# Relu attention on one core: scores and sums grouped by key block, four products for seven

## The reference

```python
Q = jnp.einsum('bnd,hed->bhne', x, Wq)          # 8 heads, 128 wide
K = jnp.einsum('bnd,hed->bhne', x, Wk)
V = jnp.einsum('bnd,hvd->bhnv', x, Wv)
scores = jnp.einsum('bhne,bhme->bhnm', Q, K)
causal = jnp.tril(jnp.ones((n, n), dtype=bool))
sim = jnp.where(causal, jax.nn.relu(scores), 0.0) / n      # n = 512
head_out = jnp.einsum('bhnm,bhmv->bnv', sim, V)            # summed over heads
s = x + head_out
```

## Time and profile before

| | |
|---|---|
| median of 3 runs | 770.13 us (767.93 to 770.13) |
| profiled execution, its own time | 770.88 us |
| its span, first to last instruction | 769.1 us |
| TensorE busy | 726.7 us, 94% |
| VectorE busy | 485.3 us, 63% |
| ScalarE busy | 422.8 us, 55% |
| POOL busy | 228.5 us, 30% |
| mean granted TensorE clock | 0.993 of full |

### The profile page before, as it was taken

The page is one execution under the profiler, slowest core; times in us unless marked ns, Lnnn a source line. Parts: engine busy times, 40 slices in busy tenths (PEclk is TensorE's granted clock), DMA queues, the critical chain, the costliest instruction groups (busy, mean ns, idle before and its releaser), DMA issues.

```text
span 769.1 us, 17574 instructions
## 1 busy us (share of the span) xinstructions
PE 726.7 (94%) x6166; PEld 577.8 (75%) x6172; DVE 485.3 (63%) x1084; ACT 422.8 (55%) x1540; POOL 228.5 (30%) x308
## 2 busy tenths in 40 slices
PE   4899999999999899999999999989999999999996
PEld 3677888878886677777767778868688787777866
DVE  6433333369886787777877775474655647556575
ACT  2444444432224567677666767374756647566473
POOL 1130000000003797776766761161303111010000
PEclk9999999999999999999999999899999999999999
DMA  8702000000001323333333330000000000000001
GB/s 251 290 1 57 0 0 0 0 0 0 0 1 43 91 63 74 87 88 86 81 85 78 81 92 21 1 9 11 14 4 17 7 11 1 1 0 0 0 1 56
DMA packets 26192, 32.73 MB, mean 43 GB/s; under 512 B 7184, under 2 KB 15888, under 8 KB 25488
## 3 DMA queue, kind: packets, MB, share of 16 engines
q1 hardware_dynamic: 24848, 29.27, 13.8%
q0 software_dynamic: 1280, 2.62, 1.3%
HBM read 12.98 MB, written 2.10 MB: 20 GB/s over the span
## 4 chain that ended last, share of the span: by engine, by line
PE 56%; issue 11%; POOL 10%; DVE 7%; POOLq 7%; ACT 5%; DMA 2%; DVEq 2%; SPq 1%; ACTq 0%
PE ps L733 9%; PE ps L745 9%; PE ps L1001 7%; PE ps L1061 6%; POOL early L569 5%; POOLq L577 5%; PE ps L1028 4%; PE ps L1044 4%; PE ps L720 4%; PE ps L714 4%; PE ps L1037 2%; POOL stage L576 2%; POOLq L579 2%; POOL early L588 2%; ACT stage L1301 2%
## 5 line engine op out<-in xcount | busy, mean ns | idle before, releaser
L569 POOL TENSOR_TENSOR early<-stage 128x512 f32<-128x512 f32 x64 | 91.0, 1442 | 55.4 <-DVE stage L1654 38.5
L1301 ACT ACTIVATE stage<-ps,nmB 128x128 f32<-128x128 f32 x256 | 89.9, 380 | 29.7 <-DVE nmB L1687 29.7
L1362 ACT ACTIVATE early<-ps,nmC 128x128 f32<-128x128 f32 (+1 forms) x224 | 77.5, 363 | 40.9 <-DVE dnC L1750 40.8
L745 PE MATMUL ps<-stage 128*128 128x128 f32 (+2 forms) x448 | 86.2, 321 | 1.4 <-DVE stage L1548 1.2
L733 PE MATMUL ps<-stage,early 128*128 128x128 f32 (+2 forms) x448 | 86.4, 321 | 0.0
L733 PEld LDWEIGHTS ps<-stage,early 128*128 128x128 f32 x448 | 65.2, 191 | 24.5 <-issue 15.5
L745 PEld LDWEIGHTS ps<-stage 128*128 128x128 f32 x448 | 65.5, 191 | 12.1 <-issue 1.9
L1028 PEld LDWEIGHTS ps<-stage,early 128*128 128x128 f32 x448 | 56.2, 193 | 22.6 <-issue 22.5
L1246 ACT ACTIVATE stage<-ps 128x512 f32<-128x512 f32 x64 | 31.4, 490 | 65.2 <-PE ps L733 65.2
L1543 DVE COPY stage<-ps 128x512 f32<-128x512 f32 x32 | 22.1, 692 | 69.4 <-PE ps L720 69.0
L1745 DVE TENSOR_REDUCE nmC<-ps 128x4 f32<-128x512 f32 (+1 forms) x56 | 36.4, 651 | 43.8 <-PE ps L1028 43.6
(11 more groups left out here) (199 smaller groups left out, 1486.2 us busy)
## 6 DMA issues: line engine op xcount, KB each, us to landing
early<-early SPq DMA_DIRECT2D x256, 64.0 KB, 2.0
x<-in_x SPq DMA_DIRECT2D x4, 256.0 KB, 3.5
stage<-in_cq SPq DMA_DIRECT2D x1, 1024.0 KB, 6.2
stage<-in_ck SPq DMA_DIRECT2D x1, 1024.0 KB, 8.2
stage<-in_cv SPq DMA_DIRECT2D x1, 1024.0 KB, 10.2
stage<-in_co SPq DMA_DIRECT2D x1, 1024.0 KB, 12.1
early<-in_wqk SPq DMA_DIRECT2D x1, 1024.0 KB, 14.0
xrows<-xhat SPq DMA_DIRECT2D x1, 1024.0 KB, 5.6
```

The costliest lines, as they stand in the source:

```text
L569: pool.tensor_tensor(to, a, b, (ALU.subtract, ALU.add)[f]).then_inc(rot_in, 1)
L745: t = pe.matmul(ps[:, b, q0:q1], vN[:, b % 2, m, :], simA[:, b % 2, s, at:at + q1 - q0], start=False, stop=False, skip_group_check=True)
L1301: t = act.activation(pB[:, u % 2, at, :], ps[:, 4 + h, i * P:(i + 1) * P], ACT.Exp, bias=nmB[:, u % 2, at:at + 1], accum_out=rsB[:, u % 2, ...
L1362: act.activation(pC[:, k, hg, 0:n], ps[:, 5 + k, hg * P:hg * P + n], ACT.Exp, bias=nmC[:, k, hg:hg + 1], accum_out=rsC[:, k, hg:hg + 1])
```

## The change

Step s now holds products of a whole key block: step 0 is key block 0 with all 512 queries, step 1 is key block 1 (384) and key block 3 (128), step 2 is key block 2 (256). Four products stand where seven stood, with the same ten blocks. Each bank then holds diagonal and later blocks together. ScalarE's `a_relu` takes the later blocks out (384, 256 and 128 columns), and only when it has done does VectorE's `a_diag` take the diagonal ones (one, two and one block). So ScalarE has three such instructions a unit, VectorE three in place of one, and sums s waits for VectorE alone. Where VectorE's three stand among its other steps is written out in its `head`. On TensorE, from head 1 on, `a_y` of the next unit moves ahead of sums 2 of the unit before.

```diff
-        A_STEPS = [[(m, m * P, m * P, (m + 1) * P) for m in range(BLK)],
-                   [(0, 0, P, N), (2, 3 * P, 3 * P, N)],
-                   [(1, 0, 2 * P, N)]]
+        A_STEPS = [[(0, 0, 0, N)],
+                   [(1, 0, P, N), (3, 3 * P, 3 * P, N)],
+                   [(2, 0, 2 * P, N)]]
+        A_DIAG = [(0, 1), (0, 2), (0, 1)]
+        A_REST = [(P, N), (P, 3 * P), (P, 2 * P)]
...
-                if s == 0:
-                    at_least(pe, diag_in, u)
-                else:
-                    at_least(pe, relu_in, 2 * u + s - 2)
+                at_least(pe, diag_in, 3 * u + s - 2)
...
-                    pe.wait_ge(diag_in, u + 1)
-                else:
-                    pe.wait_ge(relu_in, 2 * u + s)
+                pe.wait_ge(diag_in, 3 * u + s + 1)
...
                     a_scores(h, b, 0)
+                    if more and not first:
+                        a_y(nh, nb, at if last and b > 0 else W_NULL + 1)
                     if b > 0:
                         a_sums(h, b - 1, 2)
...
+                    if first:
+                        a_y(nh, nb, ready)
...
-                    if more:
-                        a_y(nh, nb, ready if first else at if last and b > 0 else W_NULL + 1)
...
             def a_relu(h, b, s):
                 act.wait_ge(sc_out, 3 * (4 * h + b) + s + 1)
-                n = (N, 2 * P)[s - 1]
-                act.activation(simA[:, b % 2, s, 0:n], ps[:, 4 + s, 0:n], ACT.Relu,
+                q0, q1 = A_REST[s]
+                act.activation(simA[:, b % 2, s, q0:q1], ps[:, 4 + s, q0:q1], ACT.Relu,
                                scale=1.0 / N).then_inc(relu_in, 1)
...
                 for b in range(UNITS):
+                    a_relu(h, b, 0)
                     if not (last and b == UNITS - 1):
...
-            def a_diag(h, b):
-                dve.wait_ge(sc_out, 3 * (4 * h + b) + 1)
+            def a_diag(h, b, s):
+                dve.wait_ge(relu_in, 3 * (4 * h + b) + s + 1)
...
-                    a_diag(h, b)
+                    a_diag(h, b, 0)
                     if late is not None:
                         choose(3 * (late * UNITS + b))
+                    if not first:
+                        a_diag(h, b, 1)
+                    if late is not None:
                         choose(3 * (late * UNITS + b) + 1)
                     if not (last and b == UNITS - 1):
                         a_v(*((h, b + 1) if b < UNITS - 1 else (h + 1, 0)))
+                    if first:
+                        a_diag(h, b, 1)
+                    a_diag(h, b, 2)
                     if first:
                         for k in range(b * BLK, (b + 1) * BLK):
```

More of the change, by code:

```diff
@@ L1543, in a_v @@
                 dve.tensor_copy(vN[:, b % 2], ps[:, 7, :].rearrange("p (k d) -> p k d", d=D)).then_inc(v_in, 1)
-            def a_diag(h, b):
-                dve.wait_ge(sc_out, 3 * (4 * h + b) + 1)
-                blocks = lambda t: t.rearrange("p (m n) -> p m n", n=P)
-                dve.scalar_tensor_tensor(out=blocks(simA[:, b % 2, 0, :]), in0=blocks(ps[:, 4, :]), scalar=0.0,
-                                         in1=causal[:].unsqueeze(1).broadcast_to([P, BLK, P]),
+            def a_diag(h, b, s):
+                dve.wait_ge(relu_in, 3 * (4 * h + b) + s + 1)
+                first, n = A_DIAG[s]
+                blocks = lambda t: t.rearrange("p (m n) -> p m n", n=P)[:, first:first + 3 * n - 2:3, :]
+                dve.scalar_tensor_tensor(out=blocks(simA[:, b % 2, s, :]), in0=blocks(ps[:, 4 + s, :]), scalar=0.0,
+                                         in1=causal[:].unsqueeze(1).broadcast_to([P, n, P]),
                                          op0=ALU.max, op1=ALU.mult).then_inc(diag_in, 1)
```

## The result

| | before | after | ratio, 95% interval |
|---|---|---|---|
| median | 767.93 us (5 runs, 767.49 to 770.13) | 775.20 us (5 runs, 774.09 to 778.02) | 1.0101 (1.0079 to 1.0123) |
| the same two on another chip | 768.85 us (17 runs, 766.09 to 771.26) | 777.15 us (5 runs, 775.48 to 777.81) | 1.0102 (1.0087 to 1.0118) |
| profiled executions, own time | 770.88 and 765.91 us | 778.02 and 777.15 us | |

The loss is 7.3 to 8.3 us. The forecast was 779.5, in a range of 775.5 to 784.5: the sign was right, the size too large. The forecast was built on a baseline of 770.13; that times the measured ratio is 777.9, inside the range.

What follows compares the result with a forecast made beforehand. TensorE's stream was taken to bound heads 1 to 4, but not head 0, head 5 or the step into stage B. Terms 5.3 + 0.5 + 0.2 + 3.4 = +9.4 us gave a forecast of 779.5, range 775.5 to 784.5.

Steps and rivals of the forecast that it cites:

- Head 0: Head 0: VectorE's mask of step 2 stands ahead of `xhat` and waits for ScalarE's relu; +5.3 us, bounds 1.4 and 6.5.
- Heads 1 to 4: Heads 1 to 4: sums 0 waits 0.09, units take 6.16 us against 6.13; +0.5 over 16 units, bounds -1.0 and +4.
- The race: Heads 1 to 4: TensorE's chain (4.32 us behind scores 2) against ScalarE's and VectorE's (4.41), both leading to sums 0.
- Heads 5 to 7: Heads 5 to 7 until the last unit: head 5's VectorE +0.6 us, TensorE in heads 6 and 7 -0.4; +0.2.
- Into stage B: Step into stage B: `sums(1)` 0.7 us later, `b_rope(0)` and all behind it 3.4 late, TensorE idle some 2.9; +3.4.
- a stretch at half clock: Sign of being wrong: 1.2 GHz after TensorE's idle time, which would double the 1.72 us of `b_project(1)`.
- The passes: Step 0 in scores and sums: slot of 0.86 us for 0.89, 0.06 a unit, 1.9 at most over 32 units.
- the slower race: Rival, heads 1 to 4: the relu behind the descent loses 0.25 us or more a unit; +4, 783; 12 in 100.
- the dropped slots: Rival, all units: each of twelve dropped passes gives back its slot of 0.11 us, 42 in all; 728; 1 in 100.
- a hidden loss: Rival: head 0's and stage B's delays are hidden, TensorE's stream decides everywhere; -1.9 us, 768.3; 3 in 100.
- no change: Rival: delays hidden, but the gain is eaten by the race in heads 1 to 4; 770 us; 3 in 100.
- stage B makes up its late start: Rival, stage B: slack in its POOL chain absorbs the late start; 776.1 us; one case of a 10 in 100 rival.

Runs made afterwards that it cites:

- m_head0: The changed kernel, but in head 0 VectorE's mask of step 2 stands behind xhat and the descent; 773.22 us, 1.0070 of before.
- m_best: The changed kernel with VectorE's queue reordered at every place seen late, and `b_project(1)` ahead of TensorE's sums 1; 765.61 us, 0.9967 of before.
- m_act: m_best, but in heads 5 to 7 ScalarE copies the values out in place of VectorE; 764.53 us, 0.9955 of before.
- p_wide: The kernel before with only step 0 as one product of 512 columns in place of four of 128; 765.63 us, 0.9969 of before.
- p_late: The kernel before with ten extra products ahead of stage A, their result overwritten; 775.25 us, 1.0095 of before.
- c_before: The kernel before, unchanged, profiled once more; 767.93 us, 1.0000.
- c_after: The changed kernel, run and profiled once more; 777.15 us, 1.0102 of before.

## Why the prediction was right in sign and too large

1. **The baseline, 2.2 of 4.3 us.** I took the median of three runs, 770.13. Over the later runs before's median is 767.9 to 768.9, and the execution that I profiled (770.88) had a long stage B (230.3; its repetition took 225.7). 779.5 is 4.3 above 775.20, and 770.13 - 767.93 = 2.2 is half of that. The other half is the step: +9.4 forecast, +7.3 measured, though the parts below sum to +9.1. That all parts together came so near is in part luck, since smaller errors cancel (items 2 to 5).
2. **Head 0, +5.3 for +4.9.** The mechanism is as described, link by link: exp at +3.06 (3.1), `a_y` released by `weights` after 1.45, 2.43 from exp to `a_y` (2.42). The units lost 1.28, 1.41, 1.42 and 0.87 where I had 1.38, 1.5, 1.5 and 1.1. Moving mask 2 (m_head0) gives back 2.6 of the 4.9, not all: mask 1 stands there too (0.33 a unit), in unit 0 a transfer takes over, and in unit 2 two instructions of VectorE ran longer. m_best, with `xhat` ahead of both masks, has 7.85 for units 2 and 3, under the 7.93 and 8.19 of before.
3. **Heads 1 to 4, +0.5 for +0.3.** The race is a tie at 4.32 (I had 4.41 against 4.32): most units are 6.10. What I gave a rival in a clause, the loop's branch, adds 0.17 or 0.18 at three turns; the 0.43 in which VectorE stands still in head 1 adds 0.35 once, and with it one unit is over the 6.3 that I had named as a sign of being wrong. m_best has the mask behind `descend`, and neither is left.
4. **Heads 5 to 7, +0.2 for 0.0.** Head 5 came as said (6.35 apart for 6.32, +0.6 for +0.5). The unit into head 5 gained 0.5 that I had at nothing: VectorE's first mask there waited 0.45 for TensorE before the change (at 163.30 us) and now waits for nothing (at 169.39). One unit of head 6 took 6.48; it is 6.07 in m_act, where VectorE is relieved, so VectorE's queue made it.
5. **Into stage B, +3.4 for +3.9 at `add(1)`.** `sums(1)` costs 0.7 as said, the idle time is 2.9 for 2.69. What I listed only as a way to be wrong happened: a stretch at half clock. It costs 0.6 until `add(1)` in the first profile and 1.0 in the second (5.62 and 6.07 from `b_project(1)`, 5.05 in before and in m_head0) and 1.7 until the first exp (27.37 and 25.70), since TensorE's further products, which ScalarE waits for, are slowed as well. Without it the step came as forecast: 25.70 - 23.03 + 0.7 = 3.4.
6. **The passes.** 0.07 a unit, near the 0.06 that the rows said. The Trainium skill (TensorE: Matmul & The Clock Gate, Back-to-back issue gap) has the back-to-back figures from which the prediction estimated 745; p_wide, at 765.63, speaks against them for these products.

The parts sum to +9.1 at `add(1)` and +10.2 at the first exp in the first pair, +9.0 and +9.7 in the second; the medians differ by 7.3 and 8.3. Between parts and medians stand 0.7 to 1.8 at `add(1)`, 1.4 to 2.9 at the first exp. That the clock does not fall in every execution can account for up to 1.7. Both profiles of the changed kernel have the fall, but the mean clock of every execution is known, and it says that not all have it. All fourteen profiles have at least 3.4 us at half clock between 477 and 499 us. The execution of 775.20 us, the median itself, has a mean clock of 0.997, and so has one of 775.48 on the other chip: 0.003 x 2 x 775 = 4.7 us at half clock in all, which leaves no room for a second 3.4. The other eight of the ten have 0.991 to 0.996. How much of the gap this explains is argued, not shown, and the rest stays open.

Rivals: the slower race and the dropped slots did not come, nor did a hidden loss or no change; "stage B makes up its late start" looked true in the first pair and was refuted by p_late, c_before and c_after.

## What to carry to other kernels

When work is split between two engines, ask where the second engine's new instruction stands in its queue: here nearly the whole loss came from short masks that stood or waited ahead of long chains, and reordering (the masks behind those chains, and `b_project(1)` ahead of sums 1 on TensorE) turned 1.0% slower into 0.3% faster (0.45% with the value copies on ScalarE). A wait that leaves TensorE idle for some us can cost more than itself, if the clock falls behind it. And repeat the profile of the baseline before a term of a few us is read from one pair: a stage here scattered by 4.6 us between executions of the same kernel.

## What the runs showed of the hardware

- Behind 2.7 us of idle TensorE the granted clock fell to 0.50 for about 3.4 us in three of four executions (in the first profile 1.3 us after TensorE had started again), and stayed at 1.00 in one of the same kernel.
- In head 0's first unit 3.4 us at a granted clock of 0.50 stand in three of fourteen profiled executions, and that unit takes 5.1 to 5.2 us in place of 3.8 to 3.9.
- An issue of a transfer on SyncE in stage B, 0.59 us as a rule, took up to 1.75 us in the first profile of before.
- ScalarE's first instruction behind a loop's turn starts 0.15 or 0.16 us later than elsewhere (0.35 or 0.36 behind Ln in place of 0.20).
- VectorE's mask takes 0.29 for one block of 128 columns, 0.42 for two and 0.69 for four; ScalarE's relu takes 0.28, 0.38, 0.48 and 0.60 for one to four. The rows of before had let me work out 0.29 for the mask of one block, and 0.28 and 0.49 for the relu of one and three.
